# Gate logits of a two-layer transformer kernel: which operand of the gate's matmuls is held in the array

## The chip, the cores and the metric

The kernel runs on one core of a Trainium2 chip. The metric is the device time of one execution in microseconds (us), the median of three executions; lower is better. A core has TensorE (PE) for matmuls, which reads its stationary operand with a weight load (PEld) and streams the moving operand past it, VectorE (DVE), ScalarE (ACT), GpSimd (POOL), and DMA queues that SyncE (SP) and ScalarE issue to. Matmuls write to PSUM, which DVE and ACT read.

## The reference

`x` and `ctx_4096` are 32 batches of 128 x 1024 f32. Two layers, each a cross attention and a feed forward, are added to `x` in turn. What matters here is the first layer's feed forward, whose rows are scaled by a softmax over 8 experts:

```python
def _L0_ffn_ref(x, weight, bias, gate_w, in_channel_scale, out_channel_scale):
    xf = x.reshape(-1, H)
    router_logits = xf @ gate_w.T                     # gate_w: 8 x 1024
    routing = jax.nn.softmax(router_logits, axis=1)
    in_scale = routing @ in_channel_scale
    out_scale = routing @ out_channel_scale
    wb = ste_sign(weight)
    out = xf * in_scale @ wb.T * out_scale + bias
...
x = x + _L0_xattn_ref(_layernorm(x), ctx_4096, ...)
x = x + _L0_ffn_ref(_layernorm(x), ...)
x = x + _L1_xattn_ref(_layernorm(x), ctx_4096, ...)
x = x + _L1_ffn_ref(_layernorm(x), ...)
```

## The kernel before, in words

After a set-up in which the weights are turned and split, the kernel goes through its 32 batches in a software pipeline. The order on each engine is the order of its own block of code; semaphores are the only coupling, and no planner moves anything. In pipeline step k the engines work on three batches at once: batch k is prepared (its context is turned, its queries, keys and values computed), batch k-1 attends (the 1024 x 1024 attention of the first layer, `scores`, `prob`, `acc`), and batch k-2 goes through the chain of everything else: normalize, gate, feed forward, second attention, last feed forward. The chain's matmul results go through the two PSUM tiles `shared0` and `shared1`, each 128 x 512.

The gate's stretch of a step, on PE, is the loop over t in `body` (from line 1071). In each t PE computes one tile of query scores (line 1010), then what the chain wants at that t, then a few units of `keys_through_queries` (lines 1023 to 1027) as `KW_UNITS` deals them out:

- t = 1: `xn_1`, the normalized rows, is turned into `shared0` and `shared1` (line 990, eight transposes). ACT copies the first half to `xnT` and DVE the second (lines 637 and 776).
- t = 2: the gate. The eight 128 x 128 tiles of `xnT` are the stationary operands, and the gate's weights `gateT[:, f, 0:E]`, eight columns, the moving one. All eight matmuls add up in `shared0[:, 0:8]`, so the logits stand one batch row to a partition, as the softmax wants them. Behind the gate comes one unit of the keys (f = 7, line 1027).
- DVE takes the maximum of the logits (line 827), ACT the exponential with its sum (line 649), DVE the quotient and its split in three parts (lines 834 to 839), behind its fourth row maximum of the query scores (line 771).
- t = 4: PE turns the route (line 1087); t = 5: the input scales (line 1094); t = 6: the output scales (line 1035). Then follow the turned row maxima (line 1106) and the feed forward (lines 1040 and 1041).

`gateT` and `xnT` are plain f32. In the trace each f32 matmul stands as two weight loads and two matmuls (line 1083: 512 of each for 8 matmuls in 32 batches); a transpose, or a matmul of `float32r` operands, stands as one of each.

Of the kernel before, what the change touches and what calls it, by code (L numbers as in the profile page):

```python
# [24 lines left out]
P = 128  # L25
# [23 lines left out]
def build(nc, x, ctx_, wq0, bq0, wk0, bk0, wv0, bv0, w_ffn, b_ffn, gate, ics, ocs,  # L49
# [13 lines left out]
    with top:  # L63
# [14 lines left out]
        signT = sb("signT", [P, T, D], F32R)  # L78
        gateT = sb("gateT", [P, T, 2 * E])
        ics3 = sb("ics3", [96, D], F32R)  # L80
# [23 lines left out]
        with ExitStack() as tmp:  # L104
# [29 lines left out]
            ident_made = sem("ident_made", tmp)  # L134
            ones_made = sem("ones_made", tmp)
            small_in = sem("small_in", tmp)
            scales_in = sem("scales_in", tmp)
# [28 lines left out]
            with nc.Block() as block:  # L166
# [12 lines left out]
                @block.gpsimd  # L179
                def _(pool):  # L180
                    nc.gpsimd.memset(ident[:, :], 0.0).then_inc(ident_made, 1)
                    pool.wait_ge(ident_made, 1)
                    nc.gpsimd.affine_select(out=ident[:, :], in_=ident[:, :], compare_op=ALU.not_equal, fill=1.0,
                                            base=0, pattern=[[-1, P]], channel_multiplier=1).then_inc(ident_made, 1)
                    nc.gpsimd.memset(ones[:, :], 1.0).then_inc(ones_made, 1)
                    nc.gpsimd.memset(minus_half[:, :], -0.5)

                @block.scalar
# [38 lines left out]
                def _(dve):  # L227
# [16 lines left out]
                    for n, (kind, i) in enumerate(groups):  # L244
# [25 lines left out]
                        elif kind == "gate":  # L270
                            nc.vector.tensor_copy(gateT[:, :, :], s[:, 0:T * 2 * E].rearrange("p (t e) -> p t e", t=T))
                            last = nc.vector.tensor_copy(
# [150 lines left out]
        shift = [sb(f"shift{i}", [P, 1]) for i in range(4)]  # L423
        logit = sb("logit", [P, E])
        r_max = [sb(f"r_max{i}", [P, 1]) for i in range(3)]
        r_bias = sb("r_bias", [P, 1])
# [49 lines left out]
        kwT_done = sem("kwT_done")  # L476
        xnT_done = [None] + [sem(f"xnT_done{i}") for i in (1, 2, 3)]
        route_done = sem("route_done")
        routeT_done = sem("routeT_done")
# [86 lines left out]
        with nc.Block() as block:  # L566
# [61 lines left out]
            def _(act):  # L628
# [10 lines left out]
                def body(k, prepare, attend, chain):  # L639
                    b, a, c = k, k - 1, k - 2  # L640
                    if chain:
# [3 lines left out]
                        transposed_half(1, c)  # L645
                    if chain:

                        act.wait_ge(r_max_ready, nth(1, c, 1))
                        nc.scalar.activation(r_exp[0][:, :], shared[0][:, 0:E], ACT.Exp, bias=r_max[0][:, :],
                                             accum_out=r_sum[0][:, :]).then_inc(r_exp_ready, 1)  # L650
# [98 lines left out]
            def _(dve):  # L749
# [62 lines left out]
                def body(k, prepare, attend, chain):  # L812
# [12 lines left out]
                    if chain:  # L825
                        dve.wait_ge(route_done, nth(1, c, 1))
                        nc.vector.tensor_reduce(r_max[0][:, :], shared[0][:, 0:E], AX_X, ALU.max,
                                                negate=True).then_inc(r_max_ready, 1)
# [153 lines left out]
            def _(pe):  # L982
# [86 lines left out]
                def body(k, prepare, attend, chain):  # L1069
                    b, a, c = k, k - 1, k - 2  # L1070
                    for t in range(T):
# [7 lines left out]
                        if chain and t == 2:  # L1079
                            pe.wait_ge(xnT_a_ready[1], nth(1, c, 1))  # L1080
                            pe.wait_ge(xnT_b_ready[1], nth(1, c, 1))
                            for f in range(T):
                                last = mm(shared[0][:, 0:E], xnT[:, f, :], gateT[:, f, 0:E], start=f == 0, stop=f == T - 1)  # L1083
                            last.then_inc(route_done, 1)
                        if chain and t == 4:
# [13 lines left out]
                        if attend:  # L1099
                            keys_through_queries(a, range(KW_UNITS[t], KW_UNITS[t + 1]))  # L1100
                        if chain and t == 6:
                            out_scale(c, 1)
# [133 lines left out]
```

## Time and profile before

| | |
|---|---|
| median of 3 executions | 2358.14 us (2357.36 to 2358.26) |
| the profiled execution | 2354.89 us |
| its span in the profile | 2353.0 us |
| PE busy | 2198.7 us (93%), 11102 matmuls |
| DVE busy | 1874.6 us (80%) |
| ACT busy | 1104.3 us (47%) |
| chain that ended last | PE 85%, ACT 4%, issue 2%, DVE 2% |
| PE by line in that chain, the gate (line 1083) | 2% |

The span is what the profile's clock covers; the execution's own time has 1.89 us around it. A busy PE counts a matmul from its start to the modelled end of its result, and matmuls overlap, so the steps from one matmul's start to the next say what a matmul costs. The chain of waits gives those steps.

### The profile page before, as it was taken

To read this page: it belongs to the slowest core of one execution; us is meant where nothing else is said; L and a number is where in the kernel's file an instruction comes from. 1 tells how busy PE (TensorE), PEld (TensorE's weight loads), DVE (VectorE), ACT (ScalarE), POOL (GpSimd) and SP (SyncE) were. 2 spreads that over 40 slices of the span, in tenths; PEclk is the share of its full clock that TensorE was granted. 3 is DMA by queue.
4 is the path that set the end of the run, shared out by engine and by line. 5 is a ranking of instruction groups with operands and counts; after the bars stand their busy time and mean duration, and the time that the engine had idled before them with its cause. 6 is when DMAs were issued, how large, how long until landed. Compare 5 with 4: busy or idle time off the path is not lost.

```text
span 2353.0 us, 33856 instructions
## 1 busy us (share of the span) xinstructions
PE 2198.7 (93%) x11102; PEld 1708.4 (73%) x11102; DVE 1874.6 (80%) x3130; ACT 1104.3 (47%) x1593; POOL 258.9 (11%) x296
## 2 busy tenths in 40 slices
PE   1997999999999999999999999999999999999986
PEld 1785777777777777777777777777777777777764
DVE  1436788888888888888888888888888888888873
ACT  2004444555554544555554544555555544555541
POOL 0000111111011111111011111111111111111100
PEclk7999999999999999999999999999999999999996
DMA  8001111111111111111111111111111111111100
GB/s 239 10 1 54 37 54 36 53 53 53 36 53 45 45 53 43 46 53 53 36 53 46 44 53 53 36 53 53 38 51 53 44 45 53 36 53 53 47 16 27
DMA packets 50217, 115.58 MB, mean 49 GB/s; under 512 B 14800, under 2 KB 23248, under 8 KB 50192
## 3 DMA queue, kind: packets, MB, share of 16 engines
q1 hardware_dynamic: 38624, 113.26, 14.5%
q10 hardware_dynamic: 11568, 1.98, 0.5%
q8 instruction: 16, 0.26, 0.0%
q14 instruction: 9, 0.07, 0.0%
HBM read 81.67 MB, written 16.78 MB: 42 GB/s over the span
## 4 chain that ended last, share of the span: by engine, by line
PE 85%; ACT 4%; issue 2%; DVE 2%; DMA 0%; POOL 0%; ACTq 0%; SPq 0%; POOLq 0%; DVEq 0%
PE acc L1066 15%; PE acc L1027 10%; PE shared L1040 5%; PE shared L1041 5%; PE shared L990 5%; PE scores L1010 5%; PE scores L1055 5%; PE scores L1054 5%; PE shared L1151 3%; PE acc L1023 3%; PE acc L1024 3%; PE acc L1025 3%; PE shared L1193 3%; PE shared L1135 3%; PE scores L1162 2%; PE shared L1083 2%
## 5 line engine op out<-in xcount | busy, mean ns | idle before, releaser
L878 DVE TENSOR_TENSOR p_lo<-prob,p_hi 128x1024 fp32r<-128x1024 f32 x256 | 312.3, 1220 | 105.8 <-ACT p_hi L685 88.0
L678 ACT ACTIVATE prob<-scores 128x1024 f32<-128x1024 f32 x256 | 260.5, 1018 | 229.3 <-PE scores L1055 178.1
L771 DVE TENSOR_REDUCE neg_max<-scores 128x1 f32<-128x1024 f32 x256 | 312.2, 1220 | 65.2 <-PE scores L1010 59.8
L605 POOL TENSOR_TENSOR rstd<-var_eps,minus_half 128x1 f32<-128x1 f32 x128 | 126.9, 991 | 1908.4 <-DVE var_eps L765 1908.4
L685 ACT ACTIVATE p_hi<-prob 128x1024 fp32r<-128x1024 f32 x256 | 271.3, 1060 | 42.8 <-PE acc L1066 38.6
L1027 PE MATMUL acc<-m_whole,cT_whole 128*128 128x512 f32 x512 | 255.2, 600 | 0.0
L886 DVE TENSOR_TENSOR p_sum<-p_sum,prob 128x1024 f32<-128x1024 f32 x192 | 233.9, 1218 | 0.0
L1010 PE MATMUL scores<-k_hh,q_hl 128*128 128x512 f32 x512 | 212.7, 496 | 0.0
L1040 PE MATMUL shared<-signT,y_hi 128*128 128x512 f32 x512 | 206.8, 404 | 0.4 <-ACT oscale L667 0.4
L1041 PE MATMUL shared<-signT,y_lo 128*128 128x512 f32 x512 | 203.9, 398 | 0.0
L1054 PE MATMUL scores<-q_hl,k_hh 128*128 128x512 f32 x512 | 200.9, 392 | 1.8 <-DVE q_m L860 1.4
L1055 PE MATMUL scores<-q_m,k_l 128*128 128x512 f32 x512 | 201.7, 394 | 0.0
L1066 PE MATMUL acc<-p_hi,v_hi 128*128 128x512 f32 x512 | 171.4, 416 | 4.2 <-DVE p_lo L878 3.9
L1066 PE MATMUL acc<-p_hi,v_lo 128*128 128x512 f32 x512 | 161.6, 397 | 0.0
L1066 PE MATMUL acc<-p_lo,v_hi 128*128 128x512 f32 x512 | 161.2, 396 | 0.0
L1010 PEld LDWEIGHTS scores<-k_hh,q_hl 128*128 128x128 f32 x512 | 97.2, 190 | 79.1 <-issue 60.9
L990 PE MATMUL shared<-ident,p_sum 128*128 128x128 f32 x512 | 69.7, 280 | 57.6 <-ACT p_sum L631 57.6
L1027 PEld LDWEIGHTS acc<-m_whole,cT_whole 128*128 128x128 f32 x512 | 90.0, 190 | 38.0 <-issue 30.6
L1040 PEld LDWEIGHTS shared<-signT,y_hi 128*128 128x128 f32 x512 | 97.3, 190 | 26.2 <-DVE y_lo L794 0.9
L1054 PEld LDWEIGHTS scores<-q_hl,k_hh 128*128 128x128 f32 x512 | 96.4, 188 | 25.4 <-DVE q_m L860 1.8
L1023 PE MATMUL acc<-m_hi,cT_hi 128*128 128x512 f32 x256 | 109.9, 429 | 4.1 <-DVE cT_lo L930 2.2
L1066 PEld LDWEIGHTS acc<-p_lo,v_hi 128*128 128x128 f32 x512 | 96.4, 188 | 23.6
(215 smaller groups left out, 4354.8 us busy)
## 6 DMA issues: line engine op xcount, KB each, us to landing
c_in<-in_ctx SPq DMA_DIRECT2D x32, 512.0 KB, 3.3
xn<-in_x SPq DMA_DIRECT2D x32, 512.0 KB, 4.1
x<-in_x SPq DMA_DIRECT2D x32, 512.0 KB, 3.3
c_val<-in_ctx SPq DMA_DIRECT2D x32, 512.0 KB, 3.5
out_x<-oscale SPq DMA_DIRECT2D x32, 512.0 KB, 2.9
q_m<-q_hl SPq DMA_DIRECT2D x32, 256.0 KB, 3.1
k_hh<-k_hh SPq DMA_DIRECT2D x32, 256.0 KB, 3.5
wq_nat<-in_L_xattn_Wq SPq DMA_DIRECT2D x4, 1024.0 KB, 10.0
```

What stands on the lines that cost most here:

```text
L678: nc.scalar.activation(prob[s % 2][:, :], scores[s % 2][:, :], ACT.Exp).then_inc(exp_ready, 1)
L685: nc.scalar.activation(p_hi[s % 2][:, :], prob[s % 2][:, :], ACT.Identity).then_inc(p_hi_ready, 1)
L771: nc.vector.tensor_reduce(neg_max[:, t:t + 1], scores[t % 2][:, :], AX_X, ALU.max, negate=True).then_inc(row_max, 1)
L878: nc.vector.tensor_tensor(p_lo[s % 2][:, :], prob[s % 2][:, :], p_hi[s % 2][:, :].bitcast(F32), ALU.subtract).then_inc(p_lo_ready, 1)
L886: nc.vector.tensor_tensor(p_sum[:, :], p_sum[:, :], prob[s % 2][:, :], ALU.add).then_inc(p_summed, 1)
L1010: last = mm(scores[t % 2][:, half(h)], q_hl[:, t * P:(t + 1) * P], k_hh[:, half(h)], start=True, stop=True)
L1027: last = mm(acc[:, half(h)], cT_whole[:, f - TS, :], m_whole[:, f - TS, half(h)], start=f == 0, stop=f == T - 1)
L1040: mm(shared[h][:, :], y_hi[:, f, :], signT[:, f, half(h)], start=f == 0, stop=False)
L1041: last = mm(shared[h][:, :], y_lo[:, f, :], signT[:, f, half(h)], start=False, stop=f == T - 1)
L1054: mm(scores[s % 2][:, half(h)], k_hh[:, s * P:(s + 1) * P], q_hl[:, half(h)], start=True, stop=False)
L1055: last = mm(scores[s % 2][:, half(h)], k_l1[:, s * P:(s + 1) * P], q_m[:, half(h)], start=False, stop=True)
L1066: last = mm(acc[:, half(h)], v[:, s, :], p[s % 2][:, half(h)], start=first, stop=end)
```

## The change

The gate's operands change places. `gateT` is widened from 16 to 32 columns per tile, zero from column 8 on, and its 32-column tiles become the stationary operands; `xnT`, 128 columns a tile, is the moving one. Tile f goes to column group f mod 4 of the array (`tile_position=(0, 32 * g)`), whose output lands in the PSUM partitions 32g to 32g+31 of `shared0[:, 0:128]`; each group adds up two tiles. That leaves four partial sums, experts on partitions and batch rows on columns. ACT copies this 128 x 128 block to a new tile `gate_parts`, and one more f32 matmul, with `gate_parts` stationary and the constant `fold` moving (128 x 8, a one at partition 32g + e, column e), adds up the four parts and turns them, into `shared0[:, 128:136]`. On PE this matmul stands behind the unit of the keys of the same t, and waits for the copy. The maximum and the exponential read the new columns. In the set-up POOL clears `gateT` and makes `fold`, and DVE waits for that before it fills `gateT`.

PE, t = 2 of the loop's body, before (line 1010: query scores, 1083: the gate, 1027 and 1023 to 1025: keys):

```order
L1010 MATMUL scores0<-k_hh,q_hl 128x512 x2
L1083 MATMUL shared0<-gateT,xnT 128x8 x8
L1027 MATMUL acc<-m_whole,cT_whole 128x512
L1008 REGISTER_ALU
L1010 MATMUL scores1<-k_hh,q_hl 128x512 x2
L1023 MATMUL acc<-m_hi,cT_hi 128x512
```

And the same place in the changed program, whose line numbers are its own (1024: query scores, 1099: the gate, 1041: keys, 1120: the new matmul):

```order
L1024 MATMUL scores0<-k_hh,q_hl 128x512 x2
L1099 MATMUL shared0<-xnT,gateT 32x128 x8
L1041 MATMUL acc<-m_whole,cT_whole 128x512
L1120 MATMUL shared0<-fold,gate_parts 128x8
L1022 REGISTER_ALU
L1024 MATMUL scores1<-k_hh,q_hl 128x512 x2
L1037 MATMUL acc<-m_hi,cT_hi 128x512
```

The gate keeps its place with eight matmuls of another shape, and the new matmul stands between the unit of the keys and the next query scores. On ACT, the same place before (the row under `xnT` is the exponential):

```order
L631 ACTIVATE p_sum<-x1,shift1,rstd1 128x1024
L637 ACTIVATE xnT<-shared0 128x512
L649 ACTIVATE r_exp0,r_sum0<-shared0,r_max0 128x8
L653 ACTIVATE route3T<-shared1 96x128
L657 ACTIVATE x1<-acc 128x512
```

and in the changed program:

```order
L643 ACTIVATE p_sum<-x1,shift1,rstd1 128x1024
L649 ACTIVATE xnT<-shared0 128x512
L660 ACTIVATE gate_parts<-shared0 128x128
L663 ACTIVATE r_exp0,r_sum0<-shared0,r_max0 128x8
L667 ACTIVATE route3T<-shared1 96x128
L671 ACTIVATE x1<-acc 128x512
```

One copy of 128 x 128 has come in ahead of the exponential; DVE's order in the loop is the same.

```diff
--- before.py
+++ after.py
@@ -76,7 +76,8 @@
         bqk_col = sb("bqk_col", [P, 1])
         bv_col = sb("bv_col", [P, 1])
         signT = sb("signT", [P, T, D], F32R)
-        gateT = sb("gateT", [P, T, 2 * E])
+        gateT = sb("gateT", [P, T, 32])
+        fold = sb("fold", [P, E])
         ics3 = sb("ics3", [96, D], F32R)
         ocs3 = sb("ocs3", [96, D], F32R)
         bias_rows = sb("bias_rows", [P, D])
@@ -133,6 +134,7 @@
             zeroed = sem("zeroed", tmp)
             ident_made = sem("ident_made", tmp)
             ones_made = sem("ones_made", tmp)
+            fold_made = sem("fold_made", tmp)
             small_in = sem("small_in", tmp)
             scales_in = sem("scales_in", tmp)
             bias_rows_in = sem("bias_rows_in", tmp)
@@ -184,6 +186,12 @@
                                             base=0, pattern=[[-1, P]], channel_multiplier=1).then_inc(ident_made, 1)
                     nc.gpsimd.memset(ones[:, :], 1.0).then_inc(ones_made, 1)
                     nc.gpsimd.memset(minus_half[:, :], -0.5)
+                    nc.gpsimd.memset(gateT[:, :, :], 0.0).then_inc(fold_made, 1)
+                    nc.gpsimd.memset(fold[:, :], 0.0).then_inc(fold_made, 1)
+                    for g in range(4):
+                        pool.wait_ge(fold_made, 2 + g)
+                        nc.gpsimd.affine_select(out=fold[:, :], in_=fold[:, :], compare_op=ALU.not_equal, fill=1.0,
+                                                base=-32 * g, pattern=[[-1, E]], channel_multiplier=1).then_inc(fold_made, 1)
 
                 @block.scalar
                 def _(act):
@@ -268,7 +276,8 @@
                             nc.vector.tensor_copy(wqkT[:, :], s[:, 0:P])
                             last = nc.vector.tensor_copy(wvT[:, :], s[:, P:2 * P])
                         elif kind == "gate":
-                            nc.vector.tensor_copy(gateT[:, :, :], s[:, 0:T * 2 * E].rearrange("p (t e) -> p t e", t=T))
+                            dve.wait_ge(fold_made, 6)
+                            nc.vector.tensor_copy(gateT[:, :, 0:E], s[:, 0:T * 2 * E].rearrange("p (t e) -> p t e", t=T)[:, :, 0:E])
                             last = nc.vector.tensor_copy(
                                 lowT[:, :, HR:HR + E], s[:, 0:T * 2 * E].rearrange("p (t e) -> p t e", t=T)[:, :, E:2 * E])
                         elif kind == "low":
@@ -422,6 +431,7 @@
         rstd = [sb(f"rstd{i}", [P, 1]) for i in range(4)]
         shift = [sb(f"shift{i}", [P, 1]) for i in range(4)]
         logit = sb("logit", [P, E])
+        gate_parts = sb("gate_parts", [P, P])
         r_max = [sb(f"r_max{i}", [P, 1]) for i in range(3)]
         r_bias = sb("r_bias", [P, 1])
         r_exp = [sb(f"r_exp{i}", [P, E]) for i in range(2)]
@@ -475,6 +485,8 @@
         den_turned = sem("den_turned")
         kwT_done = sem("kwT_done")
         xnT_done = [None] + [sem(f"xnT_done{i}") for i in (1, 2, 3)]
+        gate_done = sem("gate_done")
+        gate_parts_ready = sem("gate_parts_ready")
         route_done = sem("route_done")
         routeT_done = sem("routeT_done")
         iscale_done = sem("iscale_done")
@@ -644,9 +656,11 @@
                         act.wait_ge(low_done, nth(1, c - 1, 1))
                         transposed_half(1, c)
                     if chain:
+                        act.wait_ge(gate_done, nth(1, c, 1))
+                        nc.scalar.activation(gate_parts[:, :], shared[0][:, 0:P], ACT.Identity).then_inc(gate_parts_ready, 1)
 
                         act.wait_ge(r_max_ready, nth(1, c, 1))
-                        nc.scalar.activation(r_exp[0][:, :], shared[0][:, 0:E], ACT.Exp, bias=r_max[0][:, :],
+                        nc.scalar.activation(r_exp[0][:, :], shared[0][:, P:P + E], ACT.Exp, bias=r_max[0][:, :],
                                              accum_out=r_sum[0][:, :]).then_inc(r_exp_ready, 1)
                         act.wait_ge(routeT_done, nth(1, c, 1))
                         act.wait_ge(oscale_done, nth(2, c - 1, 2))
@@ -824,7 +838,7 @@
                         row_maximum(a, 2)
                     if chain:
                         dve.wait_ge(route_done, nth(1, c, 1))
-                        nc.vector.tensor_reduce(r_max[0][:, :], shared[0][:, 0:E], AX_X, ALU.max,
+                        nc.vector.tensor_reduce(r_max[0][:, :], shared[0][:, P:P + E], AX_X, ALU.max,
                                                 negate=True).then_inc(r_max_ready, 1)
                     if attend:
                         row_maximum(a, 3)
@@ -1079,9 +1093,12 @@
                         if chain and t == 2:
                             pe.wait_ge(xnT_a_ready[1], nth(1, c, 1))
                             pe.wait_ge(xnT_b_ready[1], nth(1, c, 1))
-                            for f in range(T):
-                                last = mm(shared[0][:, 0:E], xnT[:, f, :], gateT[:, f, 0:E], start=f == 0, stop=f == T - 1)
-                            last.then_inc(route_done, 1)
+                            for r in range(2):
+                                for g in range(4):
+                                    f = 4 * r + g
+                                    last = mm(shared[0][32 * g:32 * g + 32, 0:P], gateT[:, f, :], xnT[:, f, :],
+                                              start=r == 0, stop=r == 1, tile_position=(0, 32 * g))
+                            last.then_inc(gate_done, 1)
                         if chain and t == 4:
                             pe.wait_ge(route_ready, nth(1, c, 1))
                             nc.tensor.transpose(shared[1][0:96, 0:P], route3[:, :].bitcast(F32), ident[:, :]).then_inc(routeT_done, 1)
@@ -1098,6 +1115,9 @@
                             out_scale(c, 0)
                         if attend:
                             keys_through_queries(a, range(KW_UNITS[t], KW_UNITS[t + 1]))
+                        if chain and t == 2:
+                            pe.wait_ge(gate_parts_ready, nth(1, c, 1))
+                            mm(shared[0][:, P:P + E], gate_parts[:, :], fold[:, :], start=True, stop=True).then_inc(route_done, 1)
                         if chain and t == 6:
                             out_scale(c, 1)
                     if attend:
```

## Rows read from the trace of the kernel before

**Rows 1.** The page: busy time by engine, and the chain by engine.

```profile
PE 2198.7 (93%) x11102; PEld 1708.4 (73%) x11102; DVE 1874.6 (80%) x3130; ACT 1104.3 (47%) x1593; POOL 258.9 (11%) x296
...
PE 85%; ACT 4%; issue 2%; DVE 2%; DMA 0%; POOL 0%; ACTq 0%; SPq 0%; POOLq 0%; DVEq 0%
```

**Rows 2.** Chain of waits, one gate stretch: start us, us, what.

```profile
1109.84 0.86 PE acc L1027 x2
...
1111.17 0.87 PE shared L990 x8
...
1113.76 0.47 PE scores L1010 x2
1114.23 1.68 PE shared L1083 x16
1115.91 0.96 PE acc L1027 x2
...
1119.45 0.47 PE scores L1010 x2
1119.91 0.11 PE shared L1087
1120.02 0.24 PE acc L1023
```

**Rows 3.** The gate's line: durations ns min/median/max, starts, forms; who waited.

```profile
L1083 PEld LDWEIGHTS shared<-gateT,xnT x512: 186/192/193, 256.6 to 2299.9; 128*128 128x128 f32 x171
L1083 PE MATMUL shared<-gateT,xnT x512: 170/256/257, 256.8 to 2300.0; 128*128 128x8 f32 x171
...
  DVE r_max L827: 16.3, 32
```

**Rows 4.** Two lines that turn 128 columns, same columns as rows 3.

```profile
L990 PE MATMUL shared<-ident,p_sum x512: 270/273/477, 253.8 to 2338.5; 128*128 128x128 f32 x171
...
L1106 PEld LDWEIGHTS scores<-ident,neg_max x32: 82/84/85, 208.3 to 2247.7; 128*8 128x8 f32 x32
```

**Rows 5.** Timeline of PE in the set-up: start us, us, engine, line, what.

```profile
75.49 0.22 PE L371 MATMUL setup<-wk_hi,bq_parts 128*2 128x128 f32 x1
...
76.38 0.23 PE L372 MATMUL setup<-wk_lo_whole,bq_first 128*2 128x128 f32 x1
76.44 0.45 PE L364 MATMUL setup<-wq_hi,wk_hi 128*128 128x512 f32 x1
```

**Rows 6.** Timeline of PE and its weight loads around the turned route.

```profile
1119.52 0.13 PEld L1087 LDWEIGHTS shared<-ident,route 128*96 128x96 f32 x1
1119.75 0.27 PE L1087 MATMUL shared<-ident,route 128*96 128x128 f32 x1
```

**Rows 7.** Timeline of ACT and DVE from the gate to the route; idle time before, and releaser.

```profile
1116.15 0.27 ACT L649 ACTIVATE r_exp<-shared,r_max 128x8 f32<-128x8 f32 x1 [3.91 <-DVE r_max L827]
1120.06 0.27 ACT L653 ACTIVATE route3T<-shared 96x128 fp32r<-96x128 f32 x1 [3.56 <-PE shared L1087]
...
1115.95 0.17 DVE L827 TENSOR_REDUCE r_max<-shared 128x1 f32<-128x8 f32 x1 [0.46 <-PE shared L1083]
1117.38 1.22 DVE L771 TENSOR_REDUCE neg_max<-scores 128x1 f32<-128x1024 f32 x1 [1.27 <-PE scores L1010]
...
1119.25 0.17 DVE L839 TENSOR_TENSOR route<-route 128x8 fp32r<-128x8 f32 x1
1119.95 1.22 DVE L771 TENSOR_REDUCE neg_max<-scores 128x1 f32<-128x1024 f32 x1 [0.53 <-PE scores L1010]
```

**Rows 8.** ACT copies of 128 x 128 out of PSUM, by line: busy us, mean ns, idle.

```profile
L743 ACT ACTIVATE lowT_hi<-shared 128x128 fp32r<-128x128 f32 x32 | 8.9, 277 | 40.3 <-PE shared L1199 40.3
```

**Rows 9.** Set-up: POOL's mask of ident, and DVE's copy of the gate's weights.

```profile
1.19 0.29 POOL L183 TENSOR_SCALAR_AFFINE_SELECT ident<-ident 128x128 f32<-128x128 f32 x1 [0.24 <-POOL ident L181]
...
91.30 0.28 DVE L271 COPY gateT<-setup 128x128 f32<-128x128 f32 x1
```

**Rows 10.** Who waited for whom, whole span: us in total, times, longest.

```profile
PEld scores L1106 <- DVE neg_max L771: 15.0, 32, 0.5
```

## What the change was expected to do

> **What bounds the kernel now.** I read the page first: PE is busy 93% of the span, and the chain that ended last runs over PE for 85% and over ACT for 4% [rows 1]. Then the chain itself through one gate stretch [rows 2]: the pieces follow each other on PE with no gap between them, query scores, gate, keys, query scores. So in this stretch each step that PE saves or gains moves everything behind it, as long as no other engine becomes late. The gate is one piece of 1.68 us, 16 instructions for 8 f32 matmuls, 0.105 us each. Its own line says why: the weight loads are 128 x 128, 192 ns each, the moving side has 8 columns [rows 3]. The step is that of the weight load, not of the streaming.
>
> DVE and ACT hide here. DVE waits 0.46 us for the gate before its maximum, then 1.27 us for the next query scores, then, after the route is split, 0.53 us for the ones behind; ACT has been idle for 3.91 us before the exponential and for 3.56 us before it copies the turned route [rows 7]. At the end of the stretch the turn of the row maxima waits for DVE, but only on the side of the weight loads, 15.0 us in 32 cases, about 0.47 us each, which PE covers with its last keys [rows 10].
>
> **The change part by part.**
>
> *The gate's matmuls.* 16 weight loads of 128 columns go, 1.68 us per batch. In their place come 16 loads of 32 columns and 16 matmuls that stream 128 f32 columns. The load no longer counts: one of 8 columns takes 84 ns and one of 128 takes 192 [rows 3, 4], so 24 columns more on the first come to 84 + 24 x (192 - 84)/120 = 106 ns long, and most of that is latency that the streaming covers. What counts is the streaming. The eight turns of line 990 stream 128 f32 columns each and take 0.87 us, 0.109 each [rows 2]. If the array did the 16 one after another, that would be 1.74 us, 0.06 more than before. If the column groups really work beside each other, the order of the instructions decides: each f32 matmul stands as two instructions, and both passes of one matmul use the same group. The second pass of group 0 must stream behind its first; the first pass of group 1 can stream beside that second pass, but its own second pass must again wait. So the 16 go in 9 steps (1, then seven pairs, then 1), 9 x 0.109 = 0.98 us, 0.70 less. Were there no such order, four at a time would take 4 x 0.109 = 0.44 us, 1.24 less. The trace of before holds no narrow tile at a column position, so these are bounds: 0.44 to 1.74 us, that is -1.24 to +0.06. I take 0.98: it is what two passes on one group must cost, and it leans on nothing but the step of line 990.
>
> *The new matmul.* `gate_parts` (128 x 128) stationary and 8 columns moving is the gate's old form, two instructions of 0.105 us: +0.21 us per batch. The unit of keys behind the gate took 0.96 us where the same two instructions take 0.86 elsewhere [rows 2]; that 0.10 is the exposed load after a short matmul. It leaves the keys, since a 128-column matmul now stands ahead of them, and comes back ahead of the next query scores, behind the new matmul: zero in sum.
>
> *Changing the width.* Between full-width and narrow use of the array something may have to empty. Nearest row: the turned route, a load of 96 columns between loads of 128. From the start of the query scores ahead of it to the keys behind it the pieces are 0.47 and 0.11 us, and the next key piece 0.24: all at their usual price [rows 2, 6]. Sixteen matmuls with two stationary columns in the set-up step from 75.49 to 76.38 at 0.06 each, and the full-width one behind them starts 0.06 later [rows 5]. So zero at one end. At the other end the array empties twice: a matmul of 128 columns ends 273 ns after its start and the next could start after 109, so 0.16 us each, 0.33 us per batch [rows 4]. I take zero, the value of the nearest row, and keep 0.33. The Trainium skill speaks against it: TensorEngine Tiling (Array Packing), Key Properties, says that a change of tiling mode drains TensorE. None of the rows above is sure to be such a change, since a narrow operand may well run in the full-width mode; by the page both ends would be paid, and the sum would come out 10.6 us later.
>
> *The wait for the copy.* The new matmul waits for ACT, and ACT for the gate. From the start of the last gate matmul: 0.27 until its result; 0.04 until ACT starts (the turned route ends at 1120.02, ACT starts at 1120.06) [rows 6, 7]; 0.28 for the copy [rows 8]; 0.10 from DVE's last route piece, which ends at 1119.42, to the load that waited for it at 1119.52; 0.23 from that load to its matmul [rows 6, 7]. That is 0.92 us. PE's cover is the last gate step and the keys, 0.109 + 0.86 = 0.97 us. Hidden, with 0.05 to spare. Behind the waiting load on PE stand the query scores of t = 3, and DVE's fourth row maximum waits for those; each 0.1 us of lateness would cost 3.2 us over 32 batches. ACT itself is free: it stands idle for 3.91 us there.
>
> *DVE behind it.* The logits come later within the stretch. With the gate from 1114.23 to 1115.21, keys to 1116.07 and the new matmul to 1116.28, the maximum can start at about 1116.47 and end at 1116.64; the query scores of t = 3 would be done at 1117.38 - 0.49 = 1116.89. So the 1.27 us of idle time shrinks and stays positive, the exponential (0.27 and its sum) lies beside the fourth row maximum of 1.22 us as before, and all that follows on DVE moves with PE. The load for the turned maxima keeps its distance to DVE, as both shift alike.
>
> *Set-up.* POOL gets two clears and four masks, of the kind of the 0.29 us one at 1.19 us; `gateT` is filled at 91.30 us [rows 9]. That is 89 us of cover. The copy into `gateT` halves its elements. Nothing. The last batch has no keys to hide the copy: 0.65 us, once.
>
> *The sum.* Per batch -0.70 + 0.21 = -0.49 us, times 32: -15.7 us. On the profiled execution, 2354.89 us (span 2353.0): 2339.2. The median is 3.25 us above the profiled execution, so 2342.5 us.
>
> **The rivals.**
>
> *A. One after another.* The groups do not overlap for f32 operands: place, the 16 matmuls; price, 1.74 + 0.21 - 1.68 = +0.27 us per batch, +8.6 us, 2366.8; with both emptyings 2377. It decides when a gate instruction steps at more than (1.68 - 0.21)/16 = 0.092 us; the streaming row stands at 0.109. For it: nothing in the trace of before shows two matmuls streaming at once, and every piece of the chain is a plain sum of steps. Against it: groups of 32 write other partitions and hold other weights, so nothing is shared but the source. Chance 0.26.
>
> *B. Four at a time.* Both passes of a group spread freely: 1.24 - 0.21 = 1.03 us per batch less, -33 us, 2325. The two passes in the trace alternate load and matmul with the same output, which speaks against it. The Trainium skill (TensorE: Matmul & The Clock Gate, Part 3) is for it: matmuls in different groups start some 4 ns apart and span little more than one; it does not say whether f32's two passes do so. If it is so, the copy's wait stays at 0.92 against 0.97, since it is counted from the last gate matmul, and DVE's third row maximum, done when the wait of 0.46 us before 1115.95 begins, is early enough. Chance 0.10.
>
> *C. Given back.* The groups overlap in 9 steps, but the width is changed at both ends: -0.49 + 0.33 = -0.16 us per batch, -5 us, 2353. For it: the rule above. Against it: rows 5 and 6. Chance 0.15.
>
> *D. The copy's wait takes over.* If the copy is visible to PE 0.2 us later than I count, +6.4 us on the forecast: 2349. The spare is only 0.05 us, so this shades the forecast more than it replaces it. Chance 0.07.
>
> The forecast, 9 steps and nothing at the ends, has 0.42.
>
> **How the numbers follow.** A measurement of this kernel tells about 0.2% from no change, 4.7 us. Faster by more: the forecast, B, most of D and about half of C, 0.42 + 0.10 + 0.06 + 0.08 = 0.66; slower by more: A, less a small part of it in which the streams overlap slightly, 0.24; the rest, 0.10, is within. The range goes from 2328, which leaves out most of B, to 2367, which takes in A without emptyings and leaves out A with them. The likeliest case alone would be 2337 to 2350, with up to 0.2 us of lateness or of emptying per batch.
>
> **What would show it.** In the profile after, the piece of the gate in the chain should be 0.98 us for 16 instructions; 1.74 is A, 0.44 B. Starts of its matmuls in pairs would confirm the 9 steps. The keys behind it should be 0.86 and the new matmul 0.21. A gap ahead of the first gate matmul, or a first full-width matmul that comes over 0.1 us late, is the emptying. An idle time of PE before the new matmul with ACT as releaser is D. DVE's idle before the fourth row maximum should shrink from 1.27 to about 0.25 us and stay released by PE; if the maximum of the logits is its releaser or that idle is gone, the logits have become the bound and the gain does not pass through. The forecast is wrong if the gate's piece is not shorter, or if it is and the batches still take as long.

## The result, and the profile after

| | before | changed |
|---|---|---|
| median | 2357.75 us (4 executions) | 2332.68 us (2331.49 to 2333.97, 4 executions) |
| profiled execution, span | 2354.89 us, 2353.0 us | 2332.57 us, 2330.8 us |
| chain: gate (16 instructions) | 1.68 us | 0.57 us |
| one steady batch, gate to gate | 65.93 us | 65.17 us |

The ratio is 0.9896, 95% interval 0.9879 to 0.9913: 1.0% faster. That is the forecast's direction and inside its range, but 10 us below its 2342.5, and two terms of its sum turned out wrong in opposite directions.

The chain of waits of the changed kernel through the stretch that [rows 2] show of before, with the next batch's gate (start us, us, what; 1099: gate, 1041 and 1037: keys, 1120: new matmul, 1024: query scores):

```profile
1103.09 0.47 PE scores L1024 x2
1103.56 0.57 PE shared L1099 x16
1104.13 1.05 PE acc L1041 x2
1105.19 0.12 PE shared L1120 x2
1105.31 0.56 PE scores L1024 x2
1105.87 0.24 PE acc L1037
...
1168.73 0.57 PE shared L1099 x16
```

From the start of the gate to the first of the next keys it is 2.31 us. Before it was 3.11: the gate at 1114.23, and the same chain has the keys of line 1023 at 1117.34 and the next batch's gate at 1180.16:

```profile
1117.34 0.23 PE acc L1023
...
1180.16 1.68 PE shared L1083 x16
```

So 0.80 us goes in this stretch. From this gate to the next it is 0.76 us less, and in the mean of the first thirty such periods 0.80 (65.15 us in place of 65.95, by the starts of the gate's first matmuls): nothing behind gives the saving back. Where it comes from is seen when one asks how many of the gate's instructions are in flight in short windows (windows with this line's instructions alone: stretch, length, busy us and number of instructions of PE and of its weight loads, clock, DMA):

```profile
1103.54:1103.59 0.05, 0.05 (x4) 0.05 (x8) 1.00 0.60 246
1103.65:1103.70 0.05, 0.05 (x8) 0.05 (x4) 1.00 0.60 246
1103.76:1103.81 0.05, 0.05 (x12) 0.05 (x4) 1.00 0.00 0
```

Four, eight, twelve: each window is 0.11 us later, and each time four more have started, while a matmul takes 0.27 to 0.30 us from start to result. The timeline of the same stretch (with what ended idle time):

```profile
1104.06 0.30 PEld L1041 LDWEIGHTS acc<-m_whole,cT_whole 128*128 128x128 f32 x2 [0.20 <-issue]
...
1104.20 0.28 ACT L660 ACTIVATE gate_parts<-shared 128x128 f32<-128x128 f32 x1 [2.63 <-PE shared L1099]
1104.60 0.19 PEld L1120 LDWEIGHTS shared<-fold,gate_parts 128*128 128x128 f32 x1 [0.24 <-ACT gate_parts L660]
1105.02 0.28 PE L1120 MATMUL shared<-fold,gate_parts 128*128 128x8 f32 x2
...
1105.35 0.17 DVE L841 TENSOR_REDUCE r_max<-shared 128x1 f32<-128x8 f32 x1 [0.53 <-PE shared L1120]
...
1105.90 1.22 DVE L785 TENSOR_REDUCE neg_max<-scores 128x1 f32<-128x1024 f32 x1 [0.39 <-PE scores L1024]
```

The copy is done at 1104.48, the new matmul's load starts at 1104.60 when the second of the keys starts, and its matmul streams right behind them at 1105.02: no wait on PE. DVE still has 0.39 us idle before its fourth row maximum, released by PE, where it had 1.27 [rows 7].

The last stretch gives some back. The first thirty periods, gate to gate, are together 23.9 us shorter, the span is 22.2 us shorter. The last period is 63.12 us in the records of before and 64.79 in those of after, 1.67 us longer and not 0.80 shorter. Windows of it in the changed kernel and, in the second fence, before (stretch, length, PE, PEld, DVE, ACT, POOL, granted clock, DMA):

```profile
2253.00:2257.00 4.00, 3.33 (x21) 2.42 (x20) 3.97 (x6) 0.00 (x0) 0.00 (x0) 1.00 0.04 13
2257.00:2261.00 4.00, 2.96 (x14) 2.17 (x12) 1.94 (x8) 1.60 (x3) 0.74 (x2) 0.62 0.00 0
2261.00:2265.00 4.00, 2.35 (x10) 1.99 (x11) 1.57 (x3) 1.32 (x2) 0.00 (x0) 0.50 0.00 0
```

```profile
2284.00:2288.00 4.00, 1.28 (x9) 1.08 (x10) 2.47 (x4) 2.39 (x4) 0.00 (x0) 1.00 0.00 0
2288.00:2292.00 4.00, 1.91 (x16) 1.71 (x15) 3.32 (x12) 0.39 (x2) 0.74 (x2) 1.00 0.00 0
```

In the changed kernel the granted clock fell to 0.50, that is 1.2 GHz, and the 16 matmuls of line 1213 that follow took 3.85 us in its chain:

```profile
2264.61 3.85 PE shared L1213 x16
```

The same 16 take 1.86 us in a steady batch of the changed kernel. Before, the matching 16 (line 1193) ran at 1.00 (2.4 GHz), after larger gaps of PE:

```profile
2287.82 2.09 PE L1193 MATMUL shared<-lowT,xnT 128*128 128x136 f32 x16 [0.88 <-DVE xnT L776]
```

There the clock fell only at 2293.5. The cost is more than these 16: from the chain's sums of `p_sum` (2254.72; 2279.63 before) to DVE's first step on what these 16 wrote (2268.49; 2290.87 before), it is 13.77 us in the changed kernel and 11.24 before, 2.5 us more. It happens once. Why the clock fell earlier was not settled.

### The profile page after: what moved, and what is told of

It is laid out like the page before. It is cut to its first block, busy times and chain, and to the rows that moved or that the text cites. A ratio compares the mean times of both kernels' runs of the same rounds, so it can differ in the third digit from the quotient of the medians.

```text
span 2330.8 us, 34027 instructions
## 1 busy us (share of the span) xinstructions
PE 2175.6 (93%) x11166; PEld 1668.0 (72%) x11166; DVE 1874.4 (80%) x3130; ACT 1113.5 (48%) x1625; POOL 260.2 (11%) x302
## 4 chain that ended last, share of the span: by engine, by line
PE 85%; ACT 4%; issue 2%; DVE 2%; DMA 0%; POOL 0%; ACTq 0%; SPq 0%; POOLq 0%; DVEq 0%
PE acc L1080 15%; PE acc L1041 10%; PE scores L1024 5%; PE shared L1004 5%; PE shared L1054 5%; PE shared L1055 5%; PE scores L1069 5%; PE scores L1068 5%; PE shared L1213 3%; PE shared L1171 3%; PE acc L1037 3%; PE acc L1039 3%; PE acc L1038 3%; PE shared L1155 3%; PE scores L1182 2%; PE scores L1010 2%
## 5 line engine op out<-in xcount | busy, mean ns | idle before, releaser
L1024 PE MATMUL scores<-k_hh,q_hl 128*128 128x512 f32 x512 | 202.3, 476 | 0.3 <-issue 0.3
```

The costliest lines, as they stand in the source:

```text
L1024: last = mm(scores[t % 2][:, half(h)], q_hl[:, t * P:(t + 1) * P], k_hh[:, half(h)], start=True, stop=True)
```

## The experiments

They were timed in three sets, each with the kernel before beside it (medians 2359.09, 2358.62 and 2356.65 us), so each is given as a ratio to it; the changed kernel stands at 0.9896 (0.9879 to 0.9913). The code is cut down to the lines that matter.

**one_group.** One column group in place of four; `fold` picks group 0.

```diff
-    for r in range(2):
-        for g in range(4):
-            f = 4 * r + g
-            last = mm(shared[0][32 * g:32 * g + 32, 0:P], gateT[:, f, :], xnT[:, f, :],
-                      start=r == 0, stop=r == 1, tile_position=(0, 32 * g))
+    for f in range(T):
+        last = mm(shared[0][0:32, 0:P], gateT[:, f, :], xnT[:, f, :],
+                  start=f == 0, stop=f == T - 1, tile_position=(0, 0))
```

> All eight gate matmuls go to column group 0 and add up there; fold picks that group alone. The shapes, the short weight loads, the copy and the fold stay as in the changed kernel. Theory G: streams overlap only between different column groups, so the 16 instructions step at 0.109 us, 1.74 us in place of four rounds of 0.109 (0.44): +1.31 us per batch, +42 us on 2332.7, 2375 us, slower than the kernel before. Rival S: the gain is from the short loads and the narrow operand alone, whatever the group: the gate stays at 0.57 us and the time at 2333.

Measured 2373.67 us, ratio 1.0065 (1.0048 to 1.0082). The chain, and the gate's instructions in flight:

```profile
1122.67 1.86 PE shared L1097 x16
1124.53 1.05 PE acc L1041 x2
```

```profile
1122.65:1122.70 0.05, 0.05 (x1) 0.05 (x2) 1.00 0.40 164
1122.76:1122.81 0.05, 0.05 (x2) 0.05 (x1) 1.00 1.45 492
1122.87:1122.92 0.05, 0.05 (x3) 0.05 (x1) 1.00 0.20 82
```

One more in each step in place of four, up to the three that a length of 0.27 us allows: theory G stands, and S falls. Narrowness without several groups costs 1.29 us more per batch than the change, and makes the kernel slower than before.

**wide_swap.** The same with 72 stationary columns and no tile position; the cut is against one_group.

```diff
-    last = mm(shared[0][0:32, 0:P], gateT[:, f, :], xnT[:, f, :],
-              start=f == 0, stop=f == T - 1, tile_position=(0, 0))
+    last = mm(shared[0][0:72, 0:P], gateT[:, f, :], xnT[:, f, :], start=f == 0, stop=f == T - 1)
```

> The operands are swapped as in the change, but the stationary tile has 72 columns (zero from column 8), so the array stays in its full width, with no column groups and no change of width; all eight add up in partitions 0 to 71, fold picks the first eight. Theory G: 16 streams of 0.109 us, 1.74 us, with nothing at the ends: against one_group 0.2 us per batch less (0.095 and 0.024 us ahead of the gate, 0.092 behind it in the changed kernel), 2368 us. Rival: changing the width is free, and the late first loads come from something else: same as one_group.

Measured 2365.15 us, ratio 1.0026 (1.0015 to 1.0037).

```profile
1120.40 1.75 PE shared L1097 x16
1122.15 0.86 PE acc L1041 x2
```

Against one_group the gate is 0.11 us shorter and the keys behind it 0.19: the narrow mode costs 0.30 us per batch, 9.6 us in all (8.5 between the two medians), which is nearly the 0.33 of the forecast's upper end for emptying the array twice. The expectation of 0.2 left out the keys' first weight load, 0.1 us, which is not hidden behind the last narrow matmul. The two kernels differ in two things, 32 columns against 72 and a tile position against none; which of them brings the narrow mode and its price was not tried apart. wide_swap also prices the swap alone: 16 streams of 0.109 us and the new matmul make the kernel 0.26% slower than before.

**two_groups.**

```diff
-    for r in range(2):
-        for g in range(4):
-            f = 4 * r + g
+    for r in range(4):
+        for g in range(2):
+            f = 2 * r + g
...
-                      start=r == 0, stop=r == 1, tile_position=(0, 32 * g))
+                      start=r == 0, stop=r == 3, tile_position=(0, 32 * g))
```

> The gate's eight matmuls alternate between column groups 0 and 1. Theory G: 8 rounds of two at 0.109 us, 0.87 us plus the cost of changing the width, +0.44 us per batch, +14 us, 2347 us. Rival S: 2333. If the rounds of four were made of two groups with both of their passes at once, the gate would stay at four rounds, 2333 too.

Measured 2346.75 us, ratio 0.9950 (0.9933 to 0.9966). The gate takes 1.00 us, 0.43 more than with four groups, for four more steps of 0.109: G again.

```profile
1113.14 1.00 PE shared L1099 x16
```

**group_major.** Four groups, the two tiles of a group next to each other.

```diff
-    for r in range(2):
-        for g in range(4):
+    for g in range(4):
+        for r in range(2):
```

> Same eight matmuls on the same four groups, but the two tiles of a group stand next to each other (f = 0, 4, 1, 5, ...). The forecast took it that the two passes of an f32 matmul must stream one behind the other on their group; the changed kernel shows four starts within 20 ns instead, four times. Theory G1, passes of one group are serial and matmuls keep their order: 16 instructions less 3 overlaps at the borders of groups, 13 steps of 0.109 = 1.42 us, +0.98 us per batch, +31 us, 2364. If the passes are dealt out over the groups before they are issued, but the two tiles of one group stay serial: between 0.57 and 1.0 us for the gate, 2333 to 2347. Rival: whatever four stand next to each other run at once: 2333.

Measured 2333.84 us, ratio 0.9900 (0.9883 to 0.9916), the same as the change within the noise.

```profile
1105.70 0.59 PE shared L1099 x16
1106.30 1.05 PE acc L1041 x2
```

```profile
1105.68:1105.73 0.05, 0.05 (x4) 0.05 (x8) 1.00 0.80 328
1105.79:1105.84 0.05, 0.05 (x8) 0.05 (x6) 1.00 0.20 82
```

Here the first four instructions of the program all belong to group 0, and one_group shows that a group streams one at a time. Yet four start at once. So a matmul does not wait for those ahead of it in the program when its own group is free. (The records don't name the group; that the four belong to four groups follows from one_group. The next experiment shows the order directly.) This took the ground from under the forecast's nine steps.

**unbalanced.** Tiles 0 to 3 on group 0, 4 and 5 on group 1, 6 on group 2, 7 on group 3.

```diff
+    for f in range(T):
+        g, first, final = ((0, 0, 3), (0, 0, 3), (0, 0, 3), (0, 0, 3), (1, 4, 5), (1, 4, 5), (2, 6, 6), (3, 7, 7))[f]
+        last = mm(shared[0][32 * g:32 * g + 32, 0:P], gateT[:, f, :], xnT[:, f, :],
+                  start=f == first, stop=f == final, tile_position=(0, 32 * g))
```

> The eight gate matmuls are dealt out unevenly over the four groups: tiles 0 to 3 to group 0, 4 and 5 to group 1, 6 to group 2, 7 to group 3. With the tiles of a group next to each other (group_major) the gate still took four rounds, so matmuls do not wait for the one ahead of them in the program if their group is free. Theory Q, each group works off its own row of work and the longest row counts: group 0 has 4 matmuls of 2 passes, 8 steps of 0.109 us, as with two groups: 2347 us. Rival R, any four neighbours run at once: four rounds, 2333. Rival I, matmuls start in program order and only wait for their own group: 13 steps, 2364.

Measured 2348.61 us, ratio 0.9965 (0.9952 to 0.9978): theory Q, the longest row counts; R and I fall.

```profile
1113.49 1.02 PE shared L1098 x16
```

```profile
1113.47:1113.52 0.05, 0.05 (x1) 0.05 (x2) 1.00 2.00 410
...
1113.80:1113.85 0.05, 0.05 (x3) 0.05 (x1) 1.00 0.88 328
1113.92:1113.97 0.05, 0.05 (x6) 0.05 (x7) 1.00 0.40 164
```

But the other three groups do not begin at once. For four steps only group 0 streams (three in flight), and only with its fifth instruction do the first of the others start. The starts in the records of one batch, in ns from the first, say it in full:

```
changed       0 7 13 20 | 133 140 147 153 | 243 249 256 263 | 352 358 365 372
group_major   0 13 26 40 | 133 146 160 173 | 242 255 269 282 | 351 365 378 391
unbalanced    0 | 134 | 243 | 352 | 461 467 480 487 | 570 600 614 620 | 680 710 | 789 819
```

With up to three instructions waiting behind the running one of a group, PE goes on to the next group; with more it stands. That reading fits all three rows; it was not tried with other depths.

The trace of this run also shows the order itself. One record of each gate carries the semaphore step that ends it, and that step stands on the last matmul of the program. It is the twelfth of the 16 to start, at 620 ns, in all 32 batches; four matmuls that stand ahead of it in the program start later, at 680 to 819. So starts are out of program order. The signal is not: the matmul with the step ends at 893 ns, the last of all at 1091, and ACT's copy, which waits for the step, starts at 1164, some 0.07 us behind the last of all, as in the changed kernel. In the timeline, where the gate starts at 1113.42:

```profile
1114.59 0.28 ACT L660 ACTIVATE gate_parts<-shared 128x128 f32<-128x128 f32 x1 [3.08 <-PE shared L1098]
```

**fold_first.** The new matmul right behind the gate, ahead of the keys, and no longer behind them.

```diff
                             last.then_inc(gate_done, 1)
+                            pe.wait_ge(gate_parts_ready, nth(1, c, 1))
+                            mm(shared[0][:, P:P + E], gate_parts[:, :], fold[:, :], start=True, stop=True).then_inc(route_done, 1)
```

> Only the new matmul moves: it stands right behind the gate, ahead of the unit of the keys, so nothing covers the copy. By the budget of the prediction (0.92 us from the last gate matmul's start to the new matmul, less its own step of 0.11) PE stands idle for about 0.8 us per batch, less 0.1 us of load that is no longer exposed ahead of the keys: +0.7 us, +22 us on 2332.7, 2355. Rival: DVE bounds this stretch and PE's idle time is free: 2333.

Measured 2348.51 us, ratio 0.9957 (0.9942 to 0.9971).

```profile
1112.41 0.28 ACT L660 ACTIVATE gate_parts<-shared 128x128 f32<-128x128 f32 x1 [2.63 <-PE shared L1099]
1112.74 0.30 PEld L1103 LDWEIGHTS shared<-fold,gate_parts 128*128 128x128 f32 x2 [0.67 <-ACT gate_parts L660]
1112.74 0.39 PE L1103 MATMUL shared<-fold,gate_parts 128*128 128x8 f32 x2 [0.40 <-ACT gate_parts L660]
```

The keys and the query scores behind it, in the chain:

```profile
1113.13 0.96 PE acc L1041 x2
1114.09 0.46 PE scores L1024 x2
```

The wait is real and PE pays for it, 16 us by the medians and 14 by the ratios, so the cover matters; the rival with a DVE bound falls. But it costs less than expected. From the start of the last gate matmul to the load that waits it is 0.67 us in the records, close to the budget's 0.69; the 0.23 us from the load to its matmul was too much, as only about 0.11 of it holds the matmul up. And 0.19 us of the waiting is work that the changed kernel pays anyway: the keys behind take 0.96 us here and the query scores 0.46, where they take 1.05 and 0.56 there.

**turned_fold.** One turn in place of the matmul with `fold`, and DVE adds up the groups.

```diff
-    mm(shared[0][:, P:P + E], gate_parts[:, :], fold[:, :], start=True, stop=True).then_inc(route_done, 1)
+    nc.tensor.transpose(shared[0][:, P:2 * P], gate_parts[:, :], ident[:, :]).then_inc(route_done, 1)
...
+    nc.vector.tensor_reduce(gate_logit[:, :], shared[0][:, P:2 * P].rearrange("p (g e) -> p e g", g=4)[:, 0:E, :], AX_X, ALU.add)
```

> The matmul with fold is replaced by one turn of gate_parts (one pass, 0.109 us in place of 0.225), and DVE adds up the four groups with one more reduction of 128 x 32 to 128 x 8 ahead of the maximum, about 0.17 us and 0.05 of semaphore, against 0.39 us of idle time before its fourth row maximum. If the idle time covers it: -0.1 us per batch, -3.5 us, 2329. If the reduction makes the row maximum late: 2333 or up to 2337.

Measured 2330.35 us, ratio 0.9884 (0.9867 to 0.9900). The chain shows what was meant: 0.11 and 0.46 us where the change has 0.12 and 0.56. DVE's fourth row maximum comes straight behind the maximum of the logits, so its idle time is used up to the last.

```profile
1107.42 0.11 PE shared L1123
1107.53 0.46 PE scores L1027 x2
```

```profile
1107.57 0.19 DVE L842 TENSOR_REDUCE gate_logit<-shared 128x8 f32<-128x32 f32 x1 [0.51 <-PE shared L1123]
1107.79 0.16 DVE L844 TENSOR_REDUCE r_max<-gate_logit 128x1 f32<-128x8 f32 x1
1108.02 1.22 DVE L786 TENSOR_REDUCE neg_max<-scores 128x1 f32<-128x1024 f32 x1
```

Its interval overlaps that of the change; by the medians alone the 2 us are not shown. The profiled executions show the saving in the steady batch: 65.02 us gate to gate in the mean of thirty, where the change has 65.15, the 0.1 us that was expected. Thirty batches of it make 3.8 us. The first gate of this execution starts 3.8 us later than the change's (260.57 against 256.73), behind a set-up that the edit doesn't touch, and the stretch from the 31st gate on is 2.6 us shorter, so the two medians hide where the saving is.

**den_groups.** The lesson carried to the other 16 load-bound matmuls of a batch, the sums of `p_sum`, on top of turned_fold.

```diff
-    for t in range(T):
-        last = mm(scores[1][:, t * T:(t + 1) * T], p_sum[:, t * P:(t + 1) * P], ones[:, :], start=True, stop=True)
+    for r in range(2):
+        for g in range(4):
+            t = 4 * r + g
+            last = mm(scores[1][32 * g:32 * g + 32, r * P:(r + 1) * P], ones[:, :], p_sum[:, t * P:(t + 1) * P],
+                      start=True, stop=True, tile_position=(0, 32 * g))
...
+    nc.vector.tensor_copy(den_block[:, :], scores[1][:, 0:2 * P])
...
+    for r in range(2):
+        nc.tensor.transpose(scores[1][:, HALF + r * P:HALF + (r + 1) * P], den_block[:, r * P:(r + 1) * P], ident[:, :])
...
+    nc.vector.reciprocal(den_inv[:, :], scores[1][:, HALF:HALF + 2 * P].rearrange("p (t e) -> p t e", t=T)[:, :, 0])
```

The copy stands on DVE between its two half statistics, the turns on PE ahead of the last pair of the weighing of values.

> Built on turned_fold: the sums of p_sum over its partitions (16 instructions that step at the load's 0.105 us, 1.69 us per batch) get the gate's treatment. A block of 32 columns of ones is stationary in four groups, p_sum moves, DVE copies the 128 x 256 block between its two half statistics, two turns ahead of the last pair of the weighing of values bring it back to columns, and the reciprocal reads every 32nd column. PE: 1.69 us become 0.44 + 0.32 for the width + 0.25 for the turns, -0.65 us per batch. Theory: the copy and the turns lie beside the weighing of values, so that the chain over the turned denominators starts 0.65 us earlier: -20 us, 2310. Rival: DVE, in order, is not there in time for the copy or the reciprocal and PE waits out what it saved: 2330.

Measured 2313.69 us, ratio 0.9812 (0.9797 to 0.9826): 0.8% faster than the change, and 1.9% than before. Its timeline (1207: the sums, 1103: weighing of values, 1099: the turns, 1218: turned denominators), against the kernel before's chain in the second fence (1162, 1066, 1172):

```profile
1142.52 0.64 PE L1207 MATMUL scores<-p_sum,ones 128*32 128x128 f32 x16
1143.09 0.72 PE L1103 MATMUL acc<-p_hi,v_hi 128*128 128x512 f32 x2
...
1144.11 0.43 PE L1099 MATMUL scores<-ident,den_block 128*128 128x128 f32 x2
1144.30 0.72 PE L1103 MATMUL acc<-p_lo,v_hi 128*128 128x512 f32 x2
1145.00 1.09 PE L1218 MATMUL scores<-ident,den_inv 128*128 128x128 f32 x8
```

```profile
1159.68 1.69 PE scores L1162 x16
1161.37 1.49 PE acc L1066 x6
1162.86 0.45 PE scores L1172 x4
```

From the first sum to the turned denominators it was 3.18 us and is 2.48 by the starts, but 0.1 us lies ahead of the first sum, where the narrow mode is entered: counted from the gate's first matmul, the turned denominators come 0.60 us earlier than in turned_fold, and the turns of the context behind them (line 1021) 0.55. The whole batch is 64.49 us and was 65.02. That times 32 is 17 us, the 16.7 between the two medians; the expected 0.65 us a batch was a little too much, and the difference lies in these pieces.

## Why the prediction was right, and where it was not

The forecast was 15.7 us less; the medians differ by 25.1 and the profiled executions by 22.3. The direction and the range came true although the gate's term was mis-sized by more than the whole miss, because a second wrong term went the other way. Point by point:

- **The bound.** Right. PE's chain has no gap in the stretch, and what the gate saved reached the next batch (0.80 in the stretch, 0.76 gate to gate in the chain shown).
- **The gate in nine steps, 0.98 us.** This is the step that failed: "The second pass of group 0 must stream behind its first", and so each pair would hold back the next group. The first half is right (one_group). The second is not: group_major and unbalanced show that PE lets another group's matmul start ahead of one that waits. The gate streams in four rounds, 4 x 0.109 = 0.44 us, rival B, which had 0.10.
- **Changing the width for nothing.** Also wrong, the other way: 0.30 us per batch (one_group against wide_swap), 0.11 ahead of the gate and 0.19 behind it. Rows 5 and 6 were no such change: the turns and the set-up's narrow float32r matmuls show no such cost, and the prediction had said that they might run at full width. The Trainium skill (TensorEngine Tiling (Array Packing), Key Properties) says that changing the tiling mode drains TensorE. The trace agrees that the change costs something, 0.30 us; it does not show a full emptying, since the gate's first matmul starts at 1103.49 with the query scores ahead of it ending at 1103.56, and the keys start at 1104.06 with the gate ending at 1104.13 (these ends are modelled). Nor is it 0.16 us at each end, as the prediction had worked out.
- **The rivals as exclusive cases.** A fell, with 0.57 us for the gate and not 1.74. B and C were each given a chance, and both came true at once. B's -1.03 and C's +0.33 make -0.70 us a batch, -22.4 us, 2332.5 on the profiled execution, against 2332.57 measured. The closeness is luck: a steady batch saves 0.80 us, since 0.10 of the 0.30 was an exposed load that the keys had paid before too, and the last one loses time to the clock.
- **The new matmul, 0.21 us, and the 0.10 of exposed load.** The new matmul and the load behind it are right: 0.12 us and 0.09 more on the query scores. But the 0.10 us did not leave the keys, since no full-width load was pulled ahead of the narrow mode's end. It is part of the 0.19 above.
- **The copy's wait.** Right that it is hidden; the budget of 0.92 us was too long (0.67 to the load and some 0.11 of the load itself) and the cover of 0.97 too short, as the width change adds 0.19 to it. By these numbers the spare was some 0.4 us and not 0.05, so rival D was further off than its text says. fold_first puts a price on the cover: some 15 us.
- **DVE.** Right: 0.39 us of idle time left, 0.25 forecast.
- **Set-up and last batch.** The set-up moved by 0.1 us (first load of the gate at 256.6 before, 256.7 after). The last batch's uncovered copy is there, in the chain behind the last gate (gate 0.68 us, copy 0.28, new matmul 0.40), but from the gate's start to the maximum of the logits it is 1.46 us where before it was 1.96, and from the last gate to the end of the span 54.83 where it was 54.72. What the forecast had no term for lies ahead of that gate: the 2.5 us lost where the granted clock fell earlier.

## What to carry to other kernels

A matmul with few moving columns costs its weight load, by the reading that the steps of 0.105 us bear (no run here made the load shorter and kept the 8 moving columns); with the operands swapped it costs its streaming, and gains only if the narrow outputs go to several column groups (here 1.68 us became 0.57 with four, 1.00 with two and 1.86 with one). Count the longest group rather than the order: 8 instructions in it took 1.00 us in an even deal and 1.02 in an uneven one with the longest first (with the longest last it was not tried). Add the price of entering and leaving the narrow mode, 0.30 us here, and of bringing the result back, 0.21: by these rows a burst has to save some 0.5 us before it gains, an estimate. And where two rivals touch different terms of the sum, price them together too: they can both be true.

## What the runs showed of the hardware that was not expected

- Matmuls on different column groups do not start in program order: in unbalanced the program's last matmul starts as the twelfth of 16, at 620 ns, and four that stand ahead of it start at 680 to 819. Its semaphore step still reaches ACT only when all 16 have ended, so one step on the last matmul was enough in this run. The Trainium skill (TensorE: Matmul & The Clock Gate, Part 3) says that matmuls start and end in program order; here the measurement decides against the starts, and by the recorded ends (893 ns for the program's last, 1091 for the latest) against the ends too. It also gives some 4 ns between tiles; the records show 7 ns, and 13 where four instructions of a group stand together.
- Both passes of an f32 matmul are streamed in groups like any other instruction, each 0.109 us for 128 columns.
- A group seems to hold three instructions behind the running one; a further one stops the dealing out to all groups (unbalanced).
- The narrow mode costs 0.11 us to enter and 0.19 to leave (one_group against wide_swap), of which 0.1 is a full-width weight load that nothing hides.
